# A recommender tower in one kernel: second feed-forward product with w_2 stationary in two 64-column tiles, its result copied and turned back; item/geo half of the fused layer in 64-column tiles

## The chip, the cores and the metric

The kernel runs on one core of one Trainium2 chip. The metric is device time in microseconds (us), the median of three runs. A program of this kind keeps five engines busy at once: TensorE (PE, with its weight loads as a row PEld of their own), VectorE (DVE), ScalarE (ACT), GpSimd (POOL) and SyncE (SP), which here only issues transfers.

## The reference, cut to what matters

128 sequences of 128 tokens go through three layers of width 64. Biases and constants are left out of this cut.

```python
item_emb, geo, visit = emb_table[ids], geo_table[ids], visit_table[ids]
cat = concat(gelu(item_emb @ w_item), gelu(geo @ w_geo), gelu(visit @ w_visit))
h = item_emb + 0.1 * layer_norm(gelu(cat @ w_fuse)) * (ids != 0)   # "fused layer"
h = h + attention(layernorm(h))                                     # 4 heads of 16
x = layernorm(h)
weights = x @ wr + br
sel = the 63 tokens of a sequence with the largest weights
y = gelu(sel @ w1 + b1) @ w2 + b2         # w1 64x256, w2 256x64
h = h + x + scatter(y * weights[sel])
```

The kernel computes `y` for every token and multiplies the rows that were not selected by a coefficient of zero.

## The kernel before, in words

The 128 sequences are taken in 32 groups of four (`GB`, `NG`). A group passes five stages, and step `i` of the program works on five groups at once: `a = i + 2` (gathered rows, item/geo/visit layers, fused layer), `b = i + 1` (layer norm, q, k, v), `c = i` (attention scores and exponentials), `e = i - 1` (attention values and output projection), `d = i - 2` (the feed-forward layer). Steps -2 to 3 and the last few are written out; those between are a hardware loop whose body is two steps, an even one and an odd one. There is no scheduler: each engine has its own written list of instructions per step, executes it strictly in that order, and the lists are tied by semaphores (`wait(engine, name, ...)`, `.then_inc`). So an instruction that waits holds back all that stands behind it on its engine.

What the lists hold around the change, in order:

- PE: transposes of the gathered rows (L903), of the visit rows (L911), the four score products of group c (L923), the item/geo product (L930), the visit product (L937), attention values in 32-column tiles (L867), the fused layer (L949 with `w_fv`, then two products L951 with `w_fe` and `w_fo`), transpose of x2 (L959), of the attention values (L876), of the row maxima `neg_max` (L967), q and k (L974, L979), transpose of x3 (L986), of the fused result (L999), first feed-forward product (L1009), v (L1016), transposed scores (L884, L886), transpose of the attention output (L819), second feed-forward product (`ffn_second`, L843), output projection (`project`, L833). Then comes the next step's L903.
- ACT: copies of the transposed rows (`ig_in` L462, `vi_in` L464), the gelus `cat` (L467) and `catv` (L470), the copy `pv_t` (L474), the gelu `fused` (L479), the copies `x2t` (L484) and `max_t` (L488), `q_mask` (L494), the copy `x3t` (L501), `k_hi` (L510), two gelus of the hidden layer `hid` (L516), then four exponentials `prob` (L523) with the copy `o_t` of the attention output (L455) behind the first of them.
- DVE: after the statistics of group a and the sum `W` (L775) it adds the bias to the feed-forward result and stores it (`ffn_out`, `Y`, L661), fetches indices (L677), adds the attention output to `R` (L682), then statistics, four maxima `neg_max` (L670), two normalisations `x` (L586), and so on without a break.

w_fe and w_fo are 128x128 matrices of which one half is zero: both products write all 128 partitions, and each adds only to its half. The second feed-forward product has the hidden values as stationary operand (128x128) and `w_2` as the moving one (64 columns), and its result stands with tokens on the partitions. An f32 product shows in the trace as two matmul rows; a transpose as one.

Of the kernel before, what the change touches and what calls it, by code (L numbers as in the profile page):

```python
# [32 lines left out]
ALU = mybir.AluOpType  # L33
# [33 lines left out]
    ("w_ig", P), ("w_vi", 2 * P), ("w_fe", P), ("w_fo", P), ("w_fv", P), ("w_2", 2 * D),  # L67
    ("w_o", D), ("ident", P),
    ("gamma", D), ("beta", D), ("bv", D), ("b2", D), ("wr", D), ("br", 1),
    ("b_ig", 1), ("b_vi", 1), ("b_fu", 1), ("b_q", 1), ("b_k", 1), ("b_1", 2), ("lo_row", 1),  # L70
# [8 lines left out]
def build(nc, ids, table, packed, out):  # L79
    with ExitStack() as ctx:  # L80
# [3 lines left out]
        def sem(name):  # L84
# [61 lines left out]
        hid = sb("hid", [P, 2, GT])  # L146

# [36 lines left out]
            "hid_ready", "f2_ready", "y_ready",  # L184
# [253 lines left out]
        def _(act):  # L438
# [18 lines left out]

            def step(i, odd, half):
# [46 lines left out]
                if on(b):  # L505
                    wait(act, "k_ready", 2, b)
                    if on(b - 2):
                        act.wait_ge(k_pair_in[1 - odd], (half + odd) * 64)
                    ends(act, "k_bd_in", 64, b - 2)
                    act.activation(by_row(k_hi[1 - odd][:, :]), two_banks(K_BANKS), ACT.Identity,  # L510
                                   bias=w["b_k"]).then_inc(S["kh_ready"], 1)
                if on(d):
                    ends(act, "f2_ready", 1, d - 1)
                    for m in range(2):
                        wait(act, "f1_ready", 4, d)
                        act.activation(by_row(hid[:, m, :]), two_banks((ffn_bank(d), ffn_bank(d) + 1), m),  # L516
                                       ACT.Gelu_apprx_tanh, bias=w["b_1"][:, m:m + 1]
                                       ).then_inc(S["hid_ready"], 1)
                for s in range(GB):
                    if on(c):  # L520
                        ends(act, "pv_ready", 1, c - 1)
                        wait(act, "st_ready", GB, c, s + 1)
                        act.activation(prob[:, s, :, :].rearrange("p h q -> p (h q)"),  # L523
                                       bank[SCORES[s]][:, :], ACT.Exp, scale=SCALE
                                       ).then_inc(S["prob_ready"], 1)
                    if s == 0 and on(e) and not late(i):
                        attention_out(e)

            pipeline(act, step)


        @block.vector
        def _(dve):
# [124 lines left out]
            def ffn_out(d):  # L658

                wait(dve, "f2_ready", 1, d)  # L660
                dve.tensor_tensor(  # L661
                    of(Y, d), bank[ffn_bank(d) + 1][:, 0:GB * D].rearrange("p (b d) -> p b d", b=GB),
                    w["b2"].unsqueeze(1).to_broadcast([P, GB, D]), ALU.add
                ).then_inc(S["y_ready"], 1)
# [144 lines left out]
        def _(pe):  # L809
# [28 lines left out]
            def ffn_second(d):  # L838

                wait(pe, "hid_ready", 2, d)  # L840
                for s in range(GB):
                    for m in range(2):
                        last = mm(bank[ffn_bank(d) + 1][:, s * D:(s + 1) * D],  # L843
                                  hid[:, m, slot(s)[0]], w["w_2"][:, m * D:(m + 1) * D],
                                  start=(m == 0), stop=(m == 1))
                last.then_inc(S["f2_ready"], 1)

# [44 lines left out]
            def step(i, odd, half):  # L892
# [53 lines left out]
                if on(a):  # L946
# [3 lines left out]
                    for n, wf in enumerate(("w_fe", "w_fo")):  # L950
                        last = mm(bank[6][:, 0:2 * P], w[wf],  # L951
                                  cat[:, :].rearrange("p (r s q) -> p s r q", r=2, s=2)[:, n],
                                  start=False, stop=(n == 1))
# [39 lines left out]
                if type(i) is int and i == NG + 1:  # L993
                    ffn_second(NG - 2)
                if on(a):
# [45 lines left out]
            ffn_second(NG - 1)  # L1041

# [57 lines left out]
```

## Time and profile before

| | before |
|---|---|
| median of 3 runs | 566.99 us (565.08, 566.99, 570.79) |
| the profiled execution | 564.28 us, of which the span is 562.5 us |
| PE / PEld busy | 86% / 67% |
| DVE busy | 83% |
| ACT busy | 73% |
| POOL busy | 61% |
| mean granted TensorE clock | 0.955 of 2.4 GHz |
| matmul rows | 4100 |

The span counts from the first to the last instruction of the profiled execution. Busy shares are averages over stages with different limits; a group of the timeline merges neighbouring instructions of one line, and the ends of matmuls are modelled, so that distances between starts are the safer reading on PE.

### The profile page before, as it was taken

The page shows a single profiled execution, that of the slowest core. Times are in us where ns is not written, and L with a number is a line of the kernel's source. Part 1 is how long each engine was busy: PE and PEld are TensorE (multiplying, and loading weights), DVE is VectorE, ACT ScalarE, POOL GpSimd, SP SyncE. Part 2 cuts the span into 40 slices and gives each one's busy share as a digit, 9 for nine tenths or more (in the row PEclk, how much of TensorE's full clock was granted, in tenths as well). Part 3 has the DMA queues.
Part 4 walks back from the last instruction along what each step waited for, and adds up shares of the span by engine and source line. Part 5 has one row for each costly group of instructions (what it writes and reads, how often), then busy time and mean ns, then how long its engine had stood idle before and what let it go on. Part 6 is the DMA issues. An engine that isn't in the chain of part 4 may idle for free.

```text
span 562.5 us, 14030 instructions
## 1 busy us (share of the span) xinstructions
PE 485.2 (86%) x4100; PEld 375.8 (67%) x4100; DVE 464.3 (83%) x1917; ACT 411.3 (73%) x694; POOL 342.1 (61%) x411
## 2 busy tenths in 40 slices
PE   0777788989898999999999999999999999977653
PEld 0445566767776777777777777777777777766443
DVE  5356576878798989899898989898989888898987
ACT  0326476888778888888889888888888788866830
POOL 5555365556566667666666666666766676432574
PEclk9989899899999999999999999999999999999855
DMA  3135545445555555555555555555554555444344
GB/s 102 23 69 114 96 108 102 94 94 104 110 103 98 108 109 110 114 111 112 112 115 102 109 105 112 110 111 107 107 105 101 110 113 112 105 94 96 76 112 113
DMA packets 89635, 57.74 MB, mean 103 GB/s; under 512 B 27408, under 2 KB 79248, under 8 KB 89488
## 3 DMA queue, kind: packets, MB, share of 16 engines
q1 hardware_dynamic: 83472, 47.55, 37.5%
q0 software_dynamic: 6144, 9.97, 12.4%
q8 instruction: 8, 0.13, 0.1%
q14 instruction: 11, 0.09, 0.1%
HBM read 11.08 MB, written 4.19 MB: 27 GB/s over the span
## 4 chain that ended last, share of the span: by engine, by line
PE 38%; DVE 20%; issue 19%; POOL 9%; ACT 8%; another core or an unknown queue 2%; DMA 1%; DVEq 1%; SPq 0%; ACTq 0%; POOLq 0%
PE psum L1009 5%; PE psum L930 4%; POOL rs L354 4%; PE psum L867 4%; DVE st L571 3%; PE psum L951 3%; PE psum L974 3%; PE psum L923 3%; POOL G L346 2%; PE psum L949 2%; DVE R L767 2%; PE psum L843 2%; ACT q_mask L494 2%; PE psum L903 2%
## 5 line engine op out<-in xcount | busy, mean ns | idle before, releaser
L354 POOL TENSOR_TENSOR rs<-ve,minus_half 128x4 f32<-128x4 f32 x96 | 99.6, 1037 | 130.9 <-DVE ve L581 120.3
L346 POOL DMA_INDIRECT G<-table,idx x128 | 125.5, 981 | 39.9 <-issue 35.2
L670 DVE TENSOR_REDUCE neg_max<-psum 128x4 f32<-128x512 f32 x128 | 84.3, 681 | 0.0
L523 ACT ACTIVATE prob<-psum 128x512 f32<-128x512 f32 x128 | 69.7, 611 | 0.5 <-PE psum L886 0.2
L586 DVE TENSOR_SCALAR x<-R,mv,rs 128x64 f32 (+1 forms) x256 | 66.2, 324 | 1.6 <-POOL rs L354 1.5
L843 PE MATMUL psum<-wt,hid 128*128 128x64 f32 x512 | 66.1, 285 | 0.0
L843 PEld LDWEIGHTS psum<-wt,hid 128*128 128x128 f32 x512 | 62.9, 200 | 0.5 <-ACT hid L516 0.2
L884 PE MATMUL psum<-max_row,ones_r 128*128 128x512 f32 x128 | 54.7, 428 | 0.0
L1009 PE MATMUL psum<-x3t,wt 64*128 64x256 f32 x256 | 40.1, 436 | 15.8 <-issue 8.9
L886 PEld LDWEIGHTS psum<-q_bd,k_pair 128*128 128x128 f32 x256 | 49.7, 194 | 5.8
L886 PE MATMUL psum<-q_bd,k_pair 128*128 128x256 f32 x256 | 51.9, 285 | 0.0
L728 DVE SCALAR_TENSOR_TENSOR q_s<-psum,wt,q_mask 128x512 fp32r<-128x512 f32 x32 | 24.0, 751 | 31.2 <-ACT q_mask L494 25.6
L516 ACT ACTIVATE hid<-psum,wt 128x512 f32<-128x512 f32 x64 | 40.6, 685 | 11.6 <-PE psum L1009 11.2
L516 ACT ACT_TABLE_LOAD x31 | 39.8, 1283 | 8.1 <-PE psum L1009 7.6
L571 DVE BATCH_NORM_STATS2 st<-R 128x6 f32 (+1 forms) x256 | 39.3, 216 | 3.9
L523 ACT ACT_TABLE_LOAD x32 | 41.1, 1283 | 1.9 <-PE psum L886 1.3
L930 PE MATMUL psum<-ig_in,wt 128*128 128x512 f32 x64 | 36.8, 658 | 4.9 <-DVE R L682 2.9
L1009 PEld LDWEIGHTS psum<-x3t,wt 64*128 64x128 f32 x256 | 24.0, 203 | 25.1 <-issue 14.4
L767 DVE SCALAR_TENSOR_TENSOR R<-t,rm,u 128x64 f32 (+1 forms) x128 | 35.1, 332 | 6.1 <-DVE rm L763 5.8
L923 PE MATMUL psum<-k_bd,q_s 128*128 128x512 f32 x128 | 38.9, 425 | 1.0 <-DMA k_bd<-k_hi 1.0
L479 ACT ACTIVATE fused<-psum,wt 128x256 f32<-128x256 f32 x32 | 15.2, 475 | 32.8 <-PE psum L951 27.7
L467 ACT ACT_TABLE_LOAD x30 | 38.5, 1283 | 0.5
(117 smaller groups left out, 1150.8 us busy)
## 6 DMA issues: line engine op xcount, KB each, us to landing
q_bd<-q_s SPq DMA_DIRECT2D x256, 64.0 KB
k_bd<-k_hi SPq DMA_DIRECT2D x128, 64.0 KB
k_pair<-k_hi SPq DMA_DIRECT2D x64, 128.0 KB
k_pair<-k_lo SPq DMA_DIRECT2D x64, 128.0 KB
out<-R SPq DMA_DIRECT2D x11, 256.0 KB, 2.6
G<-table,idx POOLq DMA_INDIRECT x128
wt<-packed SPq DMA_DIRECT2D x1, 1028.5 KB, 5.1
out<-R SPq DMA_DIRECT2D x2, 512.0 KB, 3.9
```

The costliest lines, as they stand in the source:

```text
L346: pool.indirect_dma_start(G[par][:, b, :], None, table, bass.IndirectOffsetOnAxis(ap=idx[par][:, b:b + 1], axis=0),).then_inc(gathered[par ...
L354: pool.tensor_tensor(rs[:, :], ve[:, :], minus_half[:, :], ALU.pow).then_inc(S[dst], 1)
L516: act.activation(by_row(hid[:, m, :]), two_banks((ffn_bank(d), ffn_bank(d) + 1), m), ACT.Gelu_apprx_tanh, bias=w["b_1"][:, m:m + 1]).then_ ...
L523: act.activation(prob[:, s, :, :].rearrange("p h q -> p (h q)"), bank[SCORES[s]][:, :], ACT.Exp, scale=SCALE).then_inc(S["prob_ready"], 1)
L571: last = dve.bn_stats(st[:, b, :], src(b))
L586: last = dve.tensor_scalar(dst[:, b, :], src(b), mv[:, b, 0:1], rs[:, b:b + 1], ALU.subtract, ALU.mult)
L670: dve.tensor_reduce(neg_max[:, HEADS * s:HEADS * s + HEADS], bank[SCORES[s]][:, :].rearrange("p (h k) -> p h k", h=HEADS), AX, ALU.max, ne ...
L843: last = mm(bank[ffn_bank(d) + 1][:, s * D:(s + 1) * D], hid[:, m, slot(s)[0]], w["w_2"][:, m * D:(m + 1) * D], start=(m == 0), stop=(m == 1))
L886: last = mm(bank[SCORES[s]][:, pair * 2 * P:(pair + 1) * 2 * P], k_pair[odd][:, pair, tok], q_bd[odd][:, at, pair, :, :].rearrange("p h q ...
L923: mm(bank[SCORES[s]][:, :], q_s[:, tok], k_bd[:, at, :, :].rearrange("p h k -> p (h k)"), start=True, stop=True).then_inc(S["s_ready"], 1)
L930: mm(bank[6][:, :], w["w_ig"], ig_in[:, :], start=True, stop=True).then_inc(S["ig_ready"], 1)
L1009: mm(bank[ffn_bank(d) + r][:, m * 2 * P:(m + 1) * 2 * P], w["w_1"][rows, m * P:(m + 1) * P], x3t[rows, :], start=True, stop=True, tile_pos ...
```

## The change

Three things, and what they need. First, `ffn_second` takes `w_2` as the stationary operand (64 columns) and the hidden values as the moving one (256 columns at a time), in two column tiles of the array: r = 0 writes partitions 0 to 63, r = 1 partitions 64 to 127. The result now has the features on the partitions. Second, ACT copies it into a new tile `y_t` and adds the bias there (`ffn_copy`), PE turns it back with two transposes (`ffn_back`), and DVE's `ffn_out` is a copy that waits for these. Third, the item/geo half of the fused layer uses one 128x64 matrix `w_f` in two column tiles in place of `w_fe` and `w_fo`. The packed constants shrink from 2057 to 1802 columns.

```diff
@@ act @@
+            def ffn_copy(d):
+                wait(act, "f2_ready", 1, d)
+                ends(act, "yb_ready", 1, d - 1)
+                act.activation(y_t[:, :], bank[ffn_bank(d) + 1][:, 0:2 * P], ACT.Identity,
+                               bias=w["b_2"]).then_inc(S["yt_ready"], 1)
...
                     if s == 0 and on(e) and not late(i):
                         attention_out(e)
+                    if s == 1 and on(d) and not late(i):
+                        ffn_copy(d)
@@ vector @@
             def ffn_out(d):
-                wait(dve, "f2_ready", 1, d)
-                dve.tensor_tensor(
-                    of(Y, d), bank[ffn_bank(d) + 1][:, 0:GB * D].rearrange("p (b d) -> p b d", b=GB),
-                    w["b2"].unsqueeze(1).to_broadcast([P, GB, D]), ALU.add
+                wait(dve, "yb_ready", 1, d)
+                dve.tensor_copy(
+                    of(Y, d), bank[ffn_bank(d) + 1][:, 0:GB * D].rearrange("p (b d) -> p b d", b=GB)
                 ).then_inc(S["y_ready"], 1)
@@ tensor @@
             def ffn_second(d):
                 wait(pe, "hid_ready", 2, d)
-                for s in range(GB):
-                    for m in range(2):
-                        last = mm(bank[ffn_bank(d) + 1][:, s * D:(s + 1) * D],
-                                  hid[:, m, slot(s)[0]], w["w_2"][:, m * D:(m + 1) * D],
-                                  start=(m == 0), stop=(m == 1))
+                for m in range(2):
+                    for r in range(2):
+                        last = mm(bank[ffn_bank(d) + 1][r * D:(r + 1) * D, 0:2 * P],
+                                  w["w_2"][:, m * D:(m + 1) * D],
+                                  hid[:, m, r * 2 * P:(r + 1) * 2 * P],
+                                  start=(m == 0), stop=(m == 1), tile_position=(0, r * D))
                 last.then_inc(S["f2_ready"], 1)
+            def ffn_back(d):
+                wait(pe, "yt_ready", 1, d)
+                for j in range(2):
+                    last = mm(bank[ffn_bank(d) + 1][:, j * P:(j + 1) * P],
+                              y_t[:, j * P:(j + 1) * P], ident, start=True, stop=True,
+                              is_transpose=True)
+                last.then_inc(S["yb_ready"], 1)
...
                     mm(bank[6][:, 0:2 * P], w["w_fv"], catv[:, :], start=True, stop=False)
-                    for n, wf in enumerate(("w_fe", "w_fo")):
-                        last = mm(bank[6][:, 0:2 * P], w[wf],
+                    for n in range(2):
+                        last = mm(bank[6][n * D:(n + 1) * D, 0:2 * P], w["w_f"],
                                   cat[:, :].rearrange("p (r s q) -> p s r q", r=2, s=2)[:, n],
-                                  start=False, stop=(n == 1))
+                                  start=False, stop=True, tile_position=(0, n * D))
...
                 if on(e) and not late(i):
                     project(e)
+                if on(d) and not late(i):
+                    ffn_back(d)
```

In the last steps (i = 32 and 33) the copy and the transposes stand directly behind the product, and the last group's `ffn_copy` and `ffn_back` end their engines' lists.

Where the new instructions stand on PE, at the end of a step in the loop. Before, with L819 the transposed attention output, L843 the second feed-forward product, L833 the projection and L903 the next step's first transposes:

```order
L819 MATMUL psum<-ident_bf,o 128x128 x3
L205 ISA
L843 MATMUL psum<-wt,hid 128x64 [waits hid_ready]
L843 MATMUL psum<-wt,hid 128x64 x7
L833 MATMUL psum<-wo_part,o_t 128x64 [waits o_t_ready]
L833 MATMUL psum<-wo_part,o_t 128x64 x11
```

The same place with the change, where L855 is the product, L845 the projection, L865 the transposes back and L925 what was L903:

```order
L855 MATMUL psum<-hid,wt 64x256 [waits hid_ready]
L855 MATMUL psum<-hid,wt 64x256 x3
L845 MATMUL psum<-wo_part,o_t 128x64 [waits o_t_ready]
L845 MATMUL psum<-wo_part,o_t 128x64 x11
L865 MATMUL psum<-wt,y_t 128x128 [waits yt_ready]
L865 MATMUL psum<-wt,y_t 128x128
L925 MATMUL psum<-wt,G 128x128 [waits v_out,gathered1]
L925 MATMUL psum<-wt,G 128x128 x3
```

Eight products of 64 columns became four of 256, and two transposes with a wait for ACT's copy now stand ahead of the next step's first instruction.

On ACT, at the end of a step in the loop, with the change (L533 is `prob`, L456 is `o_t`, L463 the new copy; before, the rows are the same without L463):

```order
L533 ACT_TABLE_LOAD
L533 ACTIVATE prob<-psum 128x512 [waits st_ready]
L456 ACTIVATE o_t<-psum 128x512 [waits ot_ready]
L206 REGISTER_ALU
L533 ACTIVATE prob<-psum 128x512 [waits st_ready]
L463 ACTIVATE y_t<-psum,wt 128x256 [waits f2_ready]
L206 REGISTER_ALU
L533 ACTIVATE prob<-psum 128x512 [waits st_ready]
```

The copy stands between the second and the third exponential, and no further table load comes with it.

On DVE, the same stretch of a step, with the change (L787 is the sum `W`, L674 what was L661, L689 and L694 what were L677 and L682):

```order
L787 TENSOR_REDUCE W<-xw 128x4
L674 REGISTER_ALU [waits yb_ready]
L674 COPY Y<-psum 128x256
L689 ISA
L689 COPY idx<-idx_all 128x4
L694 ISA [waits wo_ready]
L694 TENSOR_TENSOR R<-R,psum 128x256
```

Nothing moved there: the copy keeps the place of the addition, but the register instruction ahead of it waits for `yb_ready` (the transposes back) where it waited for `f2_ready` (the product).

## Rows read from the trace of the kernel before

**Rows 1.** The page, busy time of the engines: us, share, instructions.

```profile
PE 485.2 (86%) x4100; PEld 375.8 (67%) x4100; DVE 464.3 (83%) x1917; ACT 411.3 (73%) x694; POOL 342.1 (61%) x411
```

**Rows 2.** Timeline of ACT, 250 to 268 us: start us, us, instruction, [idle before <-releaser].

```profile
251.96 0.78 ACT L494 ACTIVATE q_mask<-psum,bq_lo,wt 128x512 fp32r<-128x512 f32 x1 [0.40 <-PE psum L974]
252.72 0.38 ACT L501 ACTIVATE x3t<-psum 128x256 f32<-128x256 f32 x1
...
255.60 1.27 ACT L516 ACTIVATE hid<-psum,wt 128x512 f32<-128x512 f32 x2 [0.61 <-PE psum L1009]
...
258.68 0.59 ACT L455 ACTIVATE o_t<-psum 128x512 bf16<-128x512 bf16 x1
259.15 1.58 ACT L523 ACTIVATE prob<-psum 128x512 f32<-128x512 f32 x3
260.63 0.60 ACT L462 ACTIVATE ig_in<-psum 128x512 f32<-128x512 f32 x1
...
265.47 0.48 ACT L479 ACTIVATE fused<-psum,wt 128x256 f32<-128x256 f32 x1 [0.86 <-PE psum L951]
...
267.05 0.78 ACT L494 ACTIVATE q_mask<-psum,bq_lo,wt 128x512 fp32r<-128x512 f32 x1 [0.55 <-PE psum L974]
```

**Rows 3.** Timeline of ACT, the following step, 267.5 to 283.5 us.

```profile
273.64 1.58 ACT L523 ACTIVATE prob<-psum 128x512 f32<-128x512 f32 x3
275.07 0.64 ACT L462 ACTIVATE ig_in<-psum 128x512 f32<-128x512 f32 x1
...
281.78 0.78 ACT L494 ACTIVATE q_mask<-psum,bq_lo,wt 128x512 fp32r<-128x512 f32 x1 [0.40 <-PE psum L974]
```

**Rows 4.** Timeline of PE, 250 to 268 us.

```profile
256.92 2.00 PE L843 MATMUL psum<-wt,hid 128*128 128x64 f32 x16
259.32 0.52 PE L833 MATMUL psum<-wo_part,o_t 65*128 65x64 bf16 x12 [0.40 <-ACT o_t L455]
259.94 0.65 PE L903 MATMUL psum<-wt,G 128*128 128x128 f32 x4
...
261.47 1.02 PE L930 MATMUL psum<-ig_in,wt 128*128 128x512 f32 x2
```

**Rows 5.** Timeline of PE, the following step, 267.5 to 283.5 us.

```profile
276.00 1.10 PE L930 MATMUL psum<-ig_in,wt 128*128 128x512 f32 x2 [0.16 <-DVE R L682]
...
277.47 1.08 PE L867 MATMUL psum<-prob,V 128*32 128x128 f32 x32
278.49 0.70 PE L949 MATMUL psum<-catv,wt 128*128 128x256 f32 x2
279.02 1.03 PE L951 MATMUL psum<-cat,wt 128*128 128x256 f32 x4
279.88 0.38 PE L959 MATMUL psum<-wt,x 128*128 128x128 f32 x2
280.10 0.60 PE L876 MATMUL psum<-wt,pv_t 128*128 128x128 f32 x4
280.75 0.33 PE L967 MATMUL psum<-wt,neg_max 128*128 128x128 f32 x1
```

**Rows 6.** Timeline of DVE, 250 to 268 us.

```profile
259.48 0.41 DVE L661 TENSOR_TENSOR Y<-psum,wt 128x256 f32 x1
...
264.21 1.28 DVE L670 TENSOR_REDUCE neg_max<-psum 128x4 f32<-128x512 f32 x2
```

**Rows 7.** Timeline of DVE, the following step, 267.5 to 283.5 us.

```profile
274.69 0.42 DVE L661 TENSOR_TENSOR Y<-psum,wt 128x256 f32 x1
...
279.41 1.28 DVE L670 TENSOR_REDUCE neg_max<-psum 128x4 f32<-128x512 f32 x2
```

**Rows 8.** Waits, whole span: engine, line <- releaser: us in total, times, longest.

```profile
DVE R L767 <- DVE rm L763: 5.8, 24, 0.2
```

**Rows 9.** Timeline of DVE, 500 to 563 us: the smallest copy out of PSUM nearby.

```profile
524.77 0.28 DVE L640 COPY coef<-psum 128x112 f32<-128x112 f32 x1 [0.41 <-PE psum L860]
```

**Rows 10.** The chain that ended last, 515 to 563 us: start us, us, what.

```profile
555.10 3.62 PE psum L843 x16
```

More of the change, by code:

```diff
@@ L66 @@
     ("w_q", P), ("w_k", P), ("w_v", P), ("w_1", HID),
-    ("w_ig", P), ("w_vi", 2 * P), ("w_fe", P), ("w_fo", P), ("w_fv", P), ("w_2", 2 * D),
+    ("w_ig", P), ("w_vi", 2 * P), ("w_f", D), ("w_fv", P), ("w_2", 2 * D),
     ("w_o", D), ("ident", P),
-    ("gamma", D), ("beta", D), ("bv", D), ("b2", D), ("wr", D), ("br", 1),
-    ("b_ig", 1), ("b_vi", 1), ("b_fu", 1), ("b_q", 1), ("b_k", 1), ("b_1", 2), ("lo_row", 1),
+    ("gamma", D), ("beta", D), ("bv", D), ("wr", D), ("br", 1),
+    ("b_ig", 1), ("b_vi", 1), ("b_fu", 1), ("b_q", 1), ("b_k", 1), ("b_1", 2), ("b_2", 1), ("lo_row", 1),
 ]
@@ L146, in build @@
         hid = sb("hid", [P, 2, GT])
+        y_t = sb("y_t", [P, 2 * P])
         wt_rank = sb("wt_rank", [P, P])
@@ L183, in build @@
             "xw_ready", "w_ready", "r_ready", "x3t_ready", "x3t_out", "f1_ready",
-            "hid_ready", "f2_ready", "y_ready",
+            "hid_ready", "f2_ready", "yt_ready", "yb_ready", "y_ready",
         )}
@@ L511, in step @@
                                    bias=w["b_k"]).then_inc(S["kh_ready"], 1)
+                if type(i) is int and i == NG + 1:
+                    ffn_copy(NG - 2)
                 if on(d):
@@ L527, in step @@
                         attention_out(e)
+                    if s == 1 and on(d) and not late(i):
+                        ffn_copy(d)
             pipeline(act, step)
+            ffn_copy(NG - 1)
         @block.vector
@@ L994, in step @@
                     ffn_second(NG - 2)
+                    ffn_back(NG - 2)
                 if on(a):
@@ L1041, in _ @@
             ffn_second(NG - 1)
+            ffn_back(NG - 1)
 def kernel(x, L0_tok_emb_table, L0_tok_geo_table, L0_tok_visit_table, L0_tok_w_item,
@@ L1070 @@
     wf = np.asarray(L0_tok_w_fuse)
-    c["w_fe"][:, :D] = c["w_fo"][:, D:] = wf[:P]
+    c["w_f"][:] = wf[:P]
     c["w_fv"][:D, :D] = c["w_fv"][D:, D:] = wf[P:]
@@ L1076 @@
     for n, src in (("gamma", L0_tok_ln_gamma), ("beta", L0_tok_ln_beta), ("bv", L0_attn_bv),
-                   ("b2", L0_ffn_b2), ("wr", L0_ffn_wr), ("br", L0_ffn_br)):
+                   ("wr", L0_ffn_wr), ("br", L0_ffn_br)):
         c[n][:] = np.asarray(src).reshape(1, -1)
     c["b_ig"][:D, 0], c["b_ig"][D:, 0] = np.asarray(L0_tok_b_item), np.asarray(L0_tok_b_geo)
-    for n, src in (("b_vi", L0_tok_b_visit), ("b_fu", L0_tok_b_fuse)):
+    for n, src in (("b_vi", L0_tok_b_visit), ("b_fu", L0_tok_b_fuse), ("b_2", L0_ffn_b2)):
         c[n][:D, 0] = c[n][D:, 0] = np.asarray(src)
```

## Prediction

> **What bounds the kernel now.** I first read the busy times of the page. PE is busy for 86% of the span, DVE for 83%, ACT for 73% [rows 1]. No engine is full, so the bound is a ring of waits, and the timelines of ACT, PE and DVE over two steps of the loop show it. The start of `q_mask` on ACT marks a step: 251.96, 267.05 and 281.78 us [rows 2, 3]. A "long" step takes 15.09, the "short" one behind it 14.73, a pair 29.82.
>
> From `q_mask` on ACT works nearly without a break to the `ig_in` of the next step. The one break is 0.61 ahead of `hid` in the long step [rows 2]. In the long step PE has finished the second feed-forward product (L843) and waits 0.40 for `o_t`; then follow L833, L903 at 259.94 and L930 at 261.47 [rows 4]. In the short step L930 waits for DVE's `R` (L682), which stands behind `Y` [rows 5, 7]. From L930 on PE's list runs through L867, L949 and L951, and `q_mask` starts 1.09 after DVE's last `neg_max` ends in the short step (279.41 + 1.28 = 280.69, then L967 at 280.75 and `q_mask` at 281.78) [rows 3, 5, 7]. So the ring is ACT from `q_mask` to `o_t`, then PE from L833 to L974, with DVE from `Y` to `neg_max` beside it and nearly as long. L843 lies beside ACT's work, not on the ring.
>
> **The second product.** An L843 row costs about 0.11: 16 of them take 2.00 with the last one's modelled end of 0.27 [rows 4]. A row of 256 moving columns costs 0.215: four L951 rows take 279.88 - 279.02 = 0.86. That column tiles run together is seen in L867: 32 rows of 128 columns take 278.49 - 277.47 = 1.02, so four tiles share eight slots of 0.11 (the spacing within L876, (0.60 - 0.27) / 3), and 0.14 is left over for changing the tiles [rows 5]. A change back also exposes a weight load: two L949 rows take 0.53, not 0.43 [rows 5]. The new product has eight rows, four slots of 0.215, so 0.86 + 0.14 + 0.14 = 1.14 against 1.84. PE saves 0.70, and pays two transposes, 0.11 each and 0.05 for the exposed first load, 0.27 together. Of the 0.70 the ring gets nothing: L833 waited for `o_t` already in the long step, and `o_t` does not come earlier.
>
> **The copy on ACT.** `y_t` reads 256 columns with a bias. The trace has no such copy; it lies between `x3t` (256 columns without bias, 0.38) and `fused` (256 with bias, a gelu, 0.48) [rows 2]. I take 0.48, since it has the bias too. The product will be ready at about 258.4, and the copy's turn comes after the second exponential: exponentials start 0.48 apart ((275.07 - 273.64) / 3 [rows 3]), so in the long step at 259.15 + 0.48 = 259.63. It is not late itself, but it starts only there, ends at 260.11, and the last two exponentials, `ig_in` and all behind them on ACT move by 0.38 (`q_mask` is followed by `x3t` after 0.76 of its 0.78, so 0.02 to 0.10 of an instruction is overlapped).
>
> **The wait on PE.** The transposes back start 0.05 after the copy, as L833 does after `o_t` (258.68 + 0.59 to 259.32), so at 260.16. L903 follows at 260.43 against 259.94, 0.49 later, and L930 0.49 later too [rows 4]. Queued behind the waiting transposes is everything of the next step on PE. ACT's `ig_in`, which needs L903, comes at the same time by either way (0.38 from ACT, 0.49 from PE).
>
> **The wait on DVE.** The second transpose starts at 260.32 and ends 0.27 later at 260.59. DVE is told after 0.05, and a register instruction stands between the wait and the copy. Where DVE has such a hand-over to itself, it costs 5.8 / 24 = 0.24 [rows 8]; I take 0.15 for both, and 0.05 to 0.24 as the bounds. So `Y` starts at 260.74, not 259.48: 1.26 later [rows 6]. In the short step the copy starts at 273.64 + 0.48 = 274.12, the transposes at 274.65, `Y` at 275.23, not 274.69: 0.54 later [rows 3, 7]. Queued behind it are `idx`, `R`, the statistics, the four maxima and both normalisations, with no idle time to take it up. `Y` as a copy instead of an addition may be cheaper than 0.41. Bounds: nothing saved, and 0.13 saved (the copy of 112 columns took 0.28 [rows 9]); I take 0.06.
>
> The Trainium skill ("VectorE: DVE Perf Modes", Why PSUM operands drop a tier) says that an f32 operand in PSUM keeps an operation at the basic rate, so a copy would save nothing. By it the sum below would be 29 x 0.06 = 1.7 higher; no row here shows a copy of this size.
>
> **The fused layer.** Four rows in 0.86 become two slots, 0.43, with 0.14 for going into the tiles and 0.14 for coming out: L959 comes 0.15 earlier, and the last product, which `fused` waits for, 0.29 earlier [rows 5]. In the loop this is worth nothing: PE reaches L967 earlier relative to L930, but `neg_max` is later still. In the four steps ahead of the first feed-forward group it is worth about 0.2 each, 0.8.
>
> **The sum.** Long step: `neg_max` ends at 264.21 + 1.28 + 1.26 - 0.06 = 266.69 [rows 6]; 1.09 later, at 267.78, comes `q_mask`, which was at 267.05: +0.73. Short step: 0.54 - 0.06 = +0.48. A pair is 1.21 longer, a step 0.605. Groups 0 to 28 meet it in the steps 2 to 30: 29 x 0.605 = 17.5. Less 0.8 for the first steps. At the end the last product, 3.62 for 16 rows at the low clock [rows 10], becomes eight slots' worth in four, 1.8 and 0.2, but 0.05 + 0.48 + 0.05 for the copy and about 0.9 for two transposes and their end come behind it: 3.5 against 3.6, nothing. The constants are 12% smaller, but PE's first instruction waits for gathered rows: nothing. Together +16.7, from 564.3 (span 562.5 and 1.8 around it) to 581.0. The median of the runs of before, 566.99, stands 2.7 above that execution, so I name 583.
>
> **Rivals.** (1) *Only PE's leg is left*: the transposes back are served so early, or `Y` is so quick, that DVE never sets L967. Then the ring is PE's: +0.49 less 0.28 for the earlier `fused` in the long step, and L903 at 274.92 with L930 1.53 behind it (as 261.47 - 259.94) at 276.45, +0.45 - 0.28 in the short one. That is 0.38 a pair, 5.5 in all, less 0.8: 569 on the profile's clock, 571.5 for the median. Against it: DVE has no idle time between `Y` and `neg_max`. (2) *Faster*: ACT takes the copy up in the 0.86 that it idles ahead of `fused` [rows 2], PE's shorter lists then pull the ring in by the 0.28 of `fused` each step: 29 x 0.28 + 0.8 = 8.9 less, 558. It decides itself at 0.28: if the copy and its waits add less than this to a step's way from `o_t` to L930, the change gains. For it: ACT is only 73% busy. Against it: the idle time lies behind L949, the copy ahead of L903, and the path between holds 0.49. (3) *The stall ahead of `hid` spreads*: 0.61 stands there in each long step only, laid to L1009 [rows 2]. With everything shifted it could stand in the short steps too: 14.5 x 0.6 = 8.7 more, 592. (4) *The column tiles of 64 do not overlap*: 0.43 more for L951 and 0.86 more for the second product, which has over 1 us in hand. L967 would then be set by PE, some 0.15 later a step: 4 more, 587. L867 speaks against it.
>
> **How the numbers follow.** My forecast has 0.55, rival 3 0.15, rival 4 0.1, rival 1 0.13, rival 2 0.07. The bounds of the unknown costs move the forecast: the hand-over to DVE by -0.1 to +0.09 a step (-2.9 to +2.6), `Y` by +1.7 to -2.0, `y_t` of 0.38 by -2.9. The range from 571 to 591 reaches to rival 1 and nearly to rival 3 and leaves out rival 2 and the rest. About 1% (5.7 us) is what a measurement of this kernel can tell from no change. Slower by more: the forecast, rivals 3 and 4 and a part of rival 1, 0.83. Within: 0.1. Faster: 0.07.
>
> **What the changed profile would show.** ACT: one more instruction of about 0.48 between the exponentials, no further table load, and no wait ahead of it. PE: a wait for ACT's `y_t` ahead of the transposes, L925 some 0.5 later after `o_t`, the second product in about 1.1. DVE: idle time ahead of `Y` of roughly 1.2 and 0.5 in turn, laid to PE's transposes, and none to speak of before. `neg_max` as the releaser of PE's transpose of the maxima in every step. A pair of steps 31.0 long. If `Y` doesn't wait, the DVE term is wrong; if `fused` comes earlier and `q_mask` with it, rival 1 or 2 holds.

## The result and the profile after

| | before | after |
|---|---|---|
| median, measured on one chip | 568.89 us (565.08 to 579.14, 4 runs) | 624.06 us (621.85 to 626.10, 4 runs) |
| ratio | | 1.108, 95% interval 1.103 to 1.114 |
| profiled execution | 564.28 us, span 562.5 us | 624.87 us, span 623.1 us |
| mean granted clock | 0.955 | 0.907 |

The ratio leaves out executions more than 1.5% above the fastest of the same kernel (of before, the one of 579.14), here and below; the medians keep them. The change costs 55 us where 16 were forecast: the direction was right, and the size lies far outside the range. The page of after, its busy times and its row of the granted clock, against [rows 1]:

```profile
PE 499.3 (80%) x3908; PEld 337.6 (54%) x3908; DVE 463.3 (74%) x1917; ACT 425.2 (68%) x726; POOL 341.5 (55%) x411
PEclk9999898797999889998999899879798998798765
```

PE is busier in microseconds (499 against 485) although it has 192 rows fewer. The clock row goes with that: it falls to 7 and 8 tenths again and again up to the end.

The table of stretches puts a number to it. Its columns are the stretch, its length, busy time and rows of PE, PEld, DVE, ACT and POOL, the mean granted clock, DMA share and GB/s. Before, then after:

```profile
113.00:500.00 387.00, 367.54 (x3281) 288.81 (x3283) 342.07 (x1465) 326.81 (x540) 250.20 (x303) 1.00 0.53 107
```

```profile
113.00:560.00 447.00, 385.65 (x3154) 264.96 (x3154) 341.41 (x1470) 339.94 (x568) 249.39 (x303) 0.92 0.47 93
```

Between two starts of `q_mask` on ACT, from the seventh step on, there are 25 steps. Before they take 375.1 us, 15.01 each. After, 18 of them take 285.2 (15.84 each) and 7 take 147.0 (21.0 each). So of 57.0 us, 25 x 0.83 = 21 are spread over all steps, and 7 x 5.16 = 36 are in seven long ones. The 3.6 left of the 60.6 between the two profiled executions lie ahead of these steps and behind them. Nine of the 18 hold some half clock too and still last 15.6 to 16.9. The forecast had 0.605 a step and no long ones.

**One of the seven**, 268.88 to 289.88 us. The clock by stretches, the step's low ones in the second and fourth row (3.4 us at 0.52 and at 0.53, which is the level of 1.2 GHz):

```profile
272.00:278.20 6.20, 4.50 (x44) 3.26 (x42) 4.05 (x17) 5.46 (x9) 3.97 (x6) 1.00 0.63 137
278.20:281.60 3.40, 3.40 (x9) 1.98 (x8) 3.23 (x19) 2.04 (x3) 1.40 (x2) 0.52 0.52 111
281.60:288.40 6.80, 4.03 (x50) 2.52 (x48) 3.37 (x12) 2.38 (x5) 4.55 (x5) 0.99 0.40 66
288.40:291.80 3.40, 3.18 (x14) 1.95 (x14) 1.23 (x3) 1.54 (x5) 0.00 (x0) 0.53 0.08 12
```

PE's timeline of after in this step, and behind the line of dots four of the same rows in the next one, whose clock is whole from 292 us on and which is undisturbed in these rows:

```profile
273.90 1.08 PE L855 MATMUL psum<-hid,wt 128*64 128x256 f32 x8
276.24 0.52 PE L845 MATMUL psum<-wo_part,o_t 65*128 65x64 bf16 x12 [1.25 <-ACT o_t L456]
277.08 0.44 PE L865 MATMUL psum<-wt,y_t 128*128 128x128 f32 x2 [0.32 <-ACT y_t L463]
277.65 0.65 PE L925 MATMUL psum<-wt,G 128*128 128x128 f32 x4
278.17 1.89 PE L945 MATMUL psum<-k_bd,q_s 128*128 128x512 f32 x4
279.86 1.91 PE L952 MATMUL psum<-ig_in,wt 128*128 128x512 f32 x2
282.21 1.08 PE L889 MATMUL psum<-prob,V 128*32 128x128 f32 x32
286.63 0.66 PE L898 MATMUL psum<-wt,pv_t 128*128 128x128 f32 x4 [1.76 <-issue]
...
298.89 1.17 PE L945 MATMUL psum<-k_bd,q_s 128*128 128x512 f32 x4
299.89 1.02 PE L952 MATMUL psum<-ig_in,wt 128*128 128x512 f32 x2
301.29 1.08 PE L889 MATMUL psum<-prob,V 128*32 128x128 f32 x32
303.79 0.60 PE L898 MATMUL psum<-wt,pv_t 128*128 128x128 f32 x4
```

Read it from the top. The new second product (L855) takes 1.08 where the old one took 2.00, and behind it PE idles 1.25 for `o_t` and 0.32 for `y_t`; before it idled 0.40 at the same place [rows 4]. Then the clock is at half: L952 starts 1.69 behind L945 instead of 1.00, and its two rows take 1.91 instead of 1.02. L889 starts 4.04 behind L945, not 2.40: PE is 1.6 late.

What comes next on GpSimd, and then on ACT, after again; the last ACT row is that of the undisturbed step:

```profile
282.42 1.08 POOL L347 DMA_INDIRECT G<-table,idx  x1 [0.19 <-issue]
...
286.31 0.95 POOL L347 DMA_INDIRECT G<-table,idx  x1 [0.30 <-issue]
```

```profile
285.98 0.60 ACT L482 ACTIVATE pv_t<-psum 128x512 f32<-128x512 f32 x1 [3.12 <-remote]
287.40 0.47 ACT L487 ACTIVATE fused<-psum,wt 128x256 f32<-128x256 f32 x1 [0.83 <-remote]
...
302.44 0.60 ACT L482 ACTIVATE pv_t<-psum 128x512 f32<-128x512 f32 x1 [0.26 <-PE psum L889]
```

L889's rows end at 283.3, and `pv_t`, which needs only them, starts at 285.98. Meanwhile GpSimd issues its four indirect transfers, the "burst" (282.42 to 287.26), and `pv_t` starts as the third of them ends (286.01). In the undisturbed step L889 ends at 302.37, before the burst that starts at 303.05, and `pv_t` follows 0.07 later. So the late L889 meets the burst and `pv_t` comes 2.6 later behind it (the idle time of 3.12 holds PE's lateness too). The long step takes 20.99, the undisturbed one 15.59. Of the 5.4 between them 0.3 is gone by the start of L945, 1.6 is the half clock up to L889, 2.6 the burst, and 0.9 lies between `pv_t` and the next `q_mask`, where the second low stretch begins (288.4 to 291.8, behind 2.9 of idle time of PE).

The table of waits of after, then two lines of before that answer to them (engine and line, total us, times, longest):

```profile
ACT pv_t L482 <- remote: 31.0, 9, 5.1
DVE Y L674 <- PE psum L865: 29.3, 30, 2.4
PE psum L845 <- ACT o_t L456: 28.8, 27, 1.3
```

```profile
PE psum L833 <- ACT o_t L455: 5.7, 13, 0.8
ACT pv_t L474 <- remote: 3.6, 1, 3.6
```

The wait for `o_t` stood in 13 steps with 0.44 each before and stands in 27 with 1.07 each after. From the seventh step on it is 1.1 to 1.3 in the steps of after that have a stall of 0.6 ahead of `hid`, and 0.4 to 0.7 in those with none. "Remote" is a releaser that the trace can't name.

### The profile page after: what moved, and what is told of

It reads as the page before. It is cut to its first block, busy times and chain, and to the rows that moved or that the text cites. A ratio compares the mean times of both kernels' runs of the same rounds, so it can differ in the third digit from the quotient of the medians.

```text
span 623.1 us, 13683 instructions
## 1 busy us (share of the span) xinstructions
PE 499.3 (80%) x3908; PEld 337.6 (54%) x3908; DVE 463.3 (74%) x1917; ACT 425.2 (68%) x726; POOL 341.5 (55%) x411
## 3 DMA queue, kind: packets, MB, share of 16 engines
q0 software_dynamic: 6144, 9.97, 11.4%
## 4 chain that ended last, share of the span: by engine, by line
PE 42%; ACT 19%; issue 17%; DVE 9%; another core or an unknown queue 6%; POOL 4%; DMA 1%; DVEq 1%; ACTq 0%; SPq 0%; POOLq 0%
PE psum L1032 8%; PE psum L945 4%; PE psum L996 4%; ACT hid L526 4%; PE psum L952 4%; ACT prob L533 4%; ACT L533 3%; PE psum L1001 2%; PE psum L889 2%; PE psum L865 2%; DVE neg_max L682 2%; PE psum L925 2%; PE psum L1008 2%; ACT y_t L463 2%
## 5 line engine op out<-in xcount | busy, mean ns | idle before, releaser
L682 DVE TENSOR_REDUCE neg_max<-psum 128x4 f32<-128x512 f32 x128 | 84.3, 681 | 0.0
L533 ACT ACTIVATE prob<-psum 128x512 f32<-128x512 f32 x128 | 73.5, 612 | 0.7 <-PE psum L908 0.4
L740 DVE SCALAR_TENSOR_TENSOR q_s<-psum,wt,q_mask 128x512 fp32r<-128x512 f32 x32 | 24.0, 751 | 35.2 <-ACT q_mask L502 24.8
L1032 PE MATMUL psum<-x3t,wt 64*128 64x256 f32 x256 | 43.3, 464 | 7.2 <-issue 4.4
L482 ACT ACTIVATE pv_t<-psum 128x512 f32<-128x512 f32 x32 | 19.1, 597 | 42.5 <-remote 31.0
L945 PE MATMUL psum<-k_bd,q_s 128*128 128x512 f32 x128 | 45.9, 489 | 0.9 <-DMA k_bd<-k_hi 0.9
L952 PE MATMUL psum<-ig_in,wt 128*128 128x512 f32 x64 | 40.1, 714 | 1.8 <-ACT ig_in L470 1.8
L845 PE MATMUL psum<-wo_part,o_t 65*128 65x64 bf16 x384 | 16.9, 194 | 28.8 <-ACT o_t L456 28.8
L502 ACT ACTIVATE q_mask<-psum,bq_lo,wt 128x512 fp32r<-128x512 f32 x32 | 24.9, 777 | 21.8 <-PE psum L996 21.1
L898 PE MATMUL psum<-wt,pv_t 128*128 128x128 f32 x128 | 20.8, 287 | 20.9 <-issue 15.6
```

Of the source, the lines that this page charges most:

```text
L682: dve.tensor_reduce(neg_max[:, HEADS * s:HEADS * s + HEADS], bank[SCORES[s]][:, :].rearrange("p (h k) -> p h k", h=HEADS), AX, ALU.max, ne ...
L945: mm(bank[SCORES[s]][:, :], q_s[:, tok], k_bd[:, at, :, :].rearrange("p h k -> p (h k)"), start=True, stop=True).then_inc(S["s_ready"], 1)
L952: mm(bank[6][:, :], w["w_ig"], ig_in[:, :], start=True, stop=True).then_inc(S["ig_ready"], 1)
L1032: mm(bank[ffn_bank(d) + r][:, m * 2 * P:(m + 1) * 2 * P], w["w_1"][rows, m * P:(m + 1) * P], x3t[rows, :], start=True, stop=True, tile_pos ...
```

## The experiments

Three theories. A: the long steps come from the clock, and the clock from the work taken off PE ahead of `o_t`. B: the long steps are a matter of the longer ring alone, or of the new wait ahead of the transposes. C: the 0.8 in every other step is the forecast's ring and, beside it, rival 3 (the stall ahead of `hid` in both steps). The kernel before is measured anew beside each group of runs; only the ratios can be set side by side from one group to another.

**The two halves of the change apart.** The fused layer alone, on the kernel before:

```diff
-                    for n, wf in enumerate(("w_fe", "w_fo")):
-                        last = mm(bank[6][:, 0:2 * P], w[wf],
+                    for n in range(2):
+                        last = mm(bank[6][n * D:(n + 1) * D, 0:2 * P], w["w_f"],
                                   cat[:, :].rearrange("p (r s q) -> p s r q", r=2, s=2)[:, n],
-                                  start=False, stop=(n == 1))
+                                  start=False, stop=True, tile_position=(0, n * D))
```

> The kernel before with the fused layer's change alone. Theory (clock): what costs 55 us is a TensorE that is idle more and whose clock then falls, together with the stalls of PE's semaphores that follow; this part takes only 0.15 us of PE's time out of a step, behind no wait, so the clock stays up between 120 and 520 us and the time is 558 to 568, some 0 to 8 us faster than before, since `fused` comes 0.29 us earlier and L967 is set by PE in every second step. Rival (tiles): the switches into and out of the 64-column tiles cost more than they save, and the time is 3 to 10 us longer.

Measured 569.91 against 564.55, ratio 1.003 (0.997 to 1.010): no difference that shows. The clock didn't stay whole as expected: the traced execution has one stretch of 6.8 us at half clock, from 328.9 us, behind 2.9 of idle time of PE ahead of L1009, in a step of 18.93.

The feed-forward part alone is the same edit taken back in the changed kernel.

> The changed kernel with the fused layer put back to w_fe and w_fo. Theory (clock): the second product, the copy on ACT and the transposes back carry the whole loss: 615 to 630 us, mean granted clock about 0.90 to 0.92, slow steps of about 21 us in between steps of 15.7. Rival (both parts needed): with 0.15 us more of PE work a step the clock stays up, the time is about 590 and the clock 0.95.

Measured 620.90 against 564.55, ratio 1.093 (1.084 to 1.102), clock 0.909. The feed-forward part carries the loss. The fused layer shows no worth either way.

**Give PE its work back, in idle time.** The changed kernel with the product, and the projection behind it, each computed twice into the same place:

```diff
+                for again in range(2):
+                    for s in range(GB):
+                        for n in range(3):
+                            last = mm(wo_bank(e)[:, s * D:(s + 1) * D],
...
+                for again in range(2):
+                    for m in range(2):
+                        for r in range(2):
+                            last = mm(bank[ffn_bank(d) + 1][r * D:(r + 1) * D, 0:2 * P],
```

> The changed kernel with the second feed-forward product computed twice over (0.86 us more PE work a step) and the output projection twice over (0.35 us more), both in places where PE waits for ACT; the second pass writes the same values. Theory (clock): PE is busy where it was idle, the clock stays up from about 120 us on, no step takes 21 us, and the time falls to 585 to 595 though PE does more. Rival (plain work): the clock has nothing to do with it, the stalls come from the order of waits; the time is 624 or, by the added work, up to 640.

Measured 583.94 against 564.55, ratio 1.035 (1.030 to 1.041). More work on PE makes the changed kernel 40 us faster (620.90 with the feed-forward part alone in the same group; 585 to 595 had been expected here). The stretch from 160 to 480 us, after and then this kernel:

```profile
160.00:480.00 320.00, 275.32 (x2272) 188.69 (x2269) 247.39 (x1063) 243.62 (x410) 183.57 (x222) 0.93 0.48 95
```

```profile
160.00:480.00 320.00, 306.23 (x2882) 213.53 (x2880) 268.25 (x1161) 268.33 (x447) 203.34 (x246) 1.00 0.51 104
```

```profile
PE psum L846 <- ACT o_t L456: 10.2, 23, 1.0
```

The clock is whole again, the wait for `o_t` is 0.44 where it stands, and no step is longer than 16.1 once the first five are past.

**Take work off PE and do nothing else.** The kernel before, with one of the two halves of the second product left out:

```diff
-                    for m in range(2):
+                    for m in range(1):
...
-                                  start=(m == 0), stop=(m == 1))
+                                  start=True, stop=True)
```

> The kernel before with one of the two halves of the second feed-forward product left out (the result misses half the hidden layer): 0.9 us less PE work a step, ahead of the wait for `o_t`, and no other change. Theory (clock): lighter PE alone brings the clock down in some windows; the time is 590 to 610 with slow steps as in the changed kernel, mean clock 0.92. Rival (the waits are to blame, ACT's copy and PE's wait for it): the product was hidden, the time stays within 3 us of before, clock 0.95.

Measured 586.09 against 564.55. The four times are 567.05, 584.39, 587.80 and 602.38, with a mean clock of 0.950, 0.925, 0.923 and 0.903, and the eleven of before lie between 560.70 and 571.08. So one execution lost nothing, three lost 20 to 38 us, and with such a spread there is no ratio; the clock falls in some executions and not in others. In the traced one (584.39) it is 0.95 from 160 to 480 us. No copy, no transposes, no wait ahead of them, and the long steps are there. One of 21.2 us, its timeline of PE, GpSimd's last transfer, and ACT:

```profile
318.22 1.10 PE L843 MATMUL psum<-wt,hid 128*128 128x64 f32 x8
320.62 0.52 PE L833 MATMUL psum<-wo_part,o_t 65*128 65x64 bf16 x12 [1.30 <-ACT o_t L455]
321.25 1.09 PE L903 MATMUL psum<-wt,G 128*128 128x128 f32 x4
322.21 2.05 PE L923 MATMUL psum<-k_bd,q_s 128*128 128x512 f32 x4
...
329.47 0.95 POOL L346 DMA_INDIRECT G<-table,idx  x1 [0.30 <-issue]
...
331.30 0.60 ACT L474 ACTIVATE pv_t<-psum 128x512 f32<-128x512 f32 x1 [4.79 <-remote]
```

The same picture: a short L843, an idle time of 1.30, then four rows of L923 in 2.05 where the same product takes 1.17 at full clock (L945 above), the burst (325.58 to 330.42), and `pv_t` 4.4 behind the end of L867's rows at 326.87. As a theory of all long steps B falls: neither the longer ring nor the wait ahead of the transposes is needed for one.

**Which idle time.** Only the product twice, and only the projection twice:

> The changed kernel with the second product computed twice, the projection once. PE's wait of 1.25 for `o_t` shrinks to 0.4, the wait of 0.33 ahead of the transposes back stays. Theory (the place where the product became short decides): no low stretch after 120 us, 580 to 587 us as with both computed twice. Rival (the two waits add up and each matters): a few slow steps, 590 to 610.

> The changed kernel with the projection computed twice, the product once: the wait ahead of the transposes back is filled, the wait of 1.25 for `o_t` stays. Theory (the short product decides): slow steps as in the changed kernel, 610 to 626. Rival (the wait ahead of the transposes decides): no slow steps, 580 to 587.

Against 565.11, the product twice gives 584.93 (1.038, 1.030 to 1.046), the projection twice 612.49 (1.085, 1.071 to 1.100). Their stretches, product first:

```profile
160.00:480.00 320.00, 300.33 (x2638) 206.76 (x2640) 267.94 (x1159) 267.75 (x445) 202.90 (x245) 1.00 0.52 104
```

```profile
160.00:480.00 320.00, 282.29 (x2548) 195.03 (x2546) 251.96 (x1083) 250.15 (x418) 189.24 (x228) 0.96 0.49 97
```

The place ahead of `o_t`, which the product fills, decides, and the 0.33 ahead of the transposes doesn't. Whether filling the latter lessens the loss isn't shown: the interval reaches from 1.071 to 1.100, and the feed-forward part alone, with that wait left open, has 1.084 to 1.102. Nor is the wait for `o_t` enough to bring the clock down each time. With the projection twice PE waits 1.1 to 1.3 in each of the seven steps from 112.7 to 222.9 us with the clock whole, and it falls only in the eighth:

```profile
113.00:222.00 109.00, 98.25 (x932) 68.74 (x930) 91.05 (x395) 91.69 (x153) 68.90 (x84) 1.00 0.51 105
222.00:244.00 22.00, 17.75 (x143) 11.90 (x142) 14.77 (x63) 13.68 (x24) 12.63 (x15) 0.89 0.49 88
```

**The copy's place and its price on ACT.** In the changed kernel, the copy directly behind `o_t` instead of one exponential later:

```diff
-                    if s == 1 and on(d) and not late(i):
+                    if s == 0 and on(d) and not late(i):
                         ffn_copy(d)
```

> The changed kernel with the copy `y_t` one exponential earlier on ACT, directly behind `o_t`. By the accounts of the prediction the transposes back then stand ready when the projection ends, L925 is hardly later than L903 was, `Y` is 0.8 later in one step and 0 in the next, and a pair of steps is 0.3 longer than before; with the stall ahead of `hid` in every step 0.9. At full clock that is 567 to 577 us. Theory (the idle time of PE brings the clock down): PE still waits 1.25 for `o_t` where the product became short, so some windows stay low: 580 to 605 us, clock 0.92 to 0.94, fewer slow steps than the changed kernel. Rival (the wait ahead of the transposes alone brought it down): no slow steps, 567 to 577.

Measured 582.26 (575.61 to 583.92) against 567.95, ratio 1.022 (1.013 to 1.032). The stretch's clock is 0.99. This is the lowest ratio of the whole change with the real gather, and the wait for `o_t` is still 24.8 us in 28 times, so that wait alone doesn't fix what the clock does. The same kernel, and the product and the projection twice:

> As the run before it, and with the second product and the projection computed twice (1.2 us more PE work a step in PE's idle places). Theory (clock): no low stretch after 120 us, steps of 15.2 to 15.4 on the mean against 15.8 of the run with the copy in its first place: 570 to 580 us. Rival (the place of the copy does not matter): 584 as there.

Measured 582.57, ratio 1.025 (1.019 to 1.031): a miss, 2.6 us above what was expected. The steps are 15.4 and 15.8, because the stall ahead of `hid` stands in nearly each of them, where the run before had it in half.

The copy alone, on the kernel before: 256 columns of `hid`, into a tile that nobody reads, behind the second exponential:

```diff
+                    if s == 1 and on(d) and not late(i):
+                        wait(act, "hid_ready", 2, d)
+                        act.activation(y_t[:, :], hid[:, 0, 0:2 * P], ACT.Identity,
+                                       bias=w["b_q"]).then_inc(S["yt_ready"], 1)
```

> The kernel before with one more copy of 256 columns with a bias on ACT (out of `hid`, into a tile that nobody reads) behind the second exponential. It prices ACT's term alone: PE and DVE wait for nothing new. By the accounts ACT's 0.38 moves `ig_in`, `cat` and `catv`, of which 0.05 to 0.25 is taken up by PE's wait ahead of L949: a step is 0.15 to 0.33 longer, 5 to 10 us in all, 569 to 574, clock 0.95. Rival (ACT is the ring by itself): 0.38 a step, 11 us, 575. Rival (any delay brings the clock down): 590 or more with slow steps.

Measured 575.29 against 567.95, ratio 1.013 (1.007 to 1.020). The copy costs 7.3 us in its place even if nobody waits for it. That lies within the 5 to 10 us that were expected, but the interval is 3.8 to 11.4 us and doesn't rule out the rival's 11.

**Without the bursts.** SyncE fetches fixed rows of the table in one plain transfer in place of GpSimd's four indirect ones, in the kernel before and in the changed one:

```diff
-                for b in range(GB):
-                    pool.indirect_dma_start(
-                        G[par][:, b, :], None, table,
...
+                sp.dma_start(G[par][:, :, :],
+                             table[0:GT, :].rearrange("(p b) f -> p b f", b=GB)
+                             ).then_inc(gathered[par], 16)
```

> The kernel before with GpSimd's four indirect transfers of a group replaced by one plain transfer of 512 fixed table rows, issued by SyncE; the gathered rows are then the wrong ones, all later work is the same. Theory (GpSimd's burst holds back PE's semaphores): the 0.61 ahead of `hid` in every second step is gone, and those steps last 14.5 to 14.7 instead of 15.1; 550 to 560 us. Rival (the stall comes from the order of PE's own work or of SyncE's transfers): it stays in every second step, 565.

> The changed kernel with the same replacement of the gather. Theory (burst): no 0.61 ahead of `hid`, and where the clock is low the step lasts 17 to 18 instead of 21, since ACT's `pv_t` no longer waits 3 us for a product that PE has issued long before: about 590 us with low stretches of the clock still there. Rival (the 21 us are the low clock alone): slow steps keep their 21 us. Second rival (the low stretches come from the burst too): no low stretch after 120 us, 575.

The kernel before without bursts takes 545.48 (2 runs), the changed one without bursts 555.72 (8 runs), and the full kernel before 549.34 in this group: ratios of 0.988 (0.974 to 1.003) and 1.014 (1.010 to 1.018). The change costs 10.2 us here. Two things stand apart from what was expected. The full kernel before is 15 to 20 us faster in this group than in the others, on a chip where it took 567.95 in the group before, and against it the plain transfer gains nothing that shows. And the theory had the changed kernel at 590 with low stretches left; it was the second rival (the low stretches come from the burst too) whose clock came true. ACT's timeline, without bursts, changed kernel: two steps, 14.92 and 15.36 long.

```profile
251.26 0.78 ACT L508 ACTIVATE q_mask<-psum,bq_lo,wt 128x512 fp32r<-128x512 f32 x1 [0.40 <-PE psum L1002]
254.29 1.27 ACT L532 ACTIVATE hid<-psum,wt 128x512 f32<-128x512 f32 x2
...
266.18 0.78 ACT L508 ACTIVATE q_mask<-psum,bq_lo,wt 128x512 fp32r<-128x512 f32 x1 [0.40 <-PE psum L1002]
269.21 1.27 ACT L532 ACTIVATE hid<-psum,wt 128x512 f32<-128x512 f32 x2
...
281.54 0.78 ACT L508 ACTIVATE q_mask<-psum,bq_lo,wt 128x512 fp32r<-128x512 f32 x1 [0.40 <-PE psum L1002]
```

Its stretch and its two waits that matter:

```profile
160.00:480.00 320.00, 291.59 (x2583) 202.07 (x2580) 277.53 (x1205) 278.88 (x467) 125.41 (x168) 1.00 0.48 107
```

```profile
PE psum L851 <- ACT o_t L462: 22.3, 31, 1.3
DVE Y L680 <- PE psum L871: 20.1, 30, 2.4
```

No stall ahead of `hid` in any step, `pv_t` laid to PE's product in all 32, no long step, and the clock whole from 40 to 490 us. PE has the same short product, but waits only 0.65 for `o_t` where it waits 1.25 in the long step above: that is the wait of the steps without the stall in the changed kernel too (0.4 to 0.7).

What the stall is worth can be read too, across groups, since no trace of the full kernels was taken in this one. The long step of the kernel before, 15.09 [rows 2], is 14.58 without bursts, its short one stays (14.73 and 14.68). The changed kernel's steps without bursts are 15.36 and 14.92. With bursts and PE filled they are 15.97 and 15.56, 0.61 and 0.64 more, and the stall ahead of `hid` stands in each. ACT's rows of that kernel:

```profile
258.29 1.27 ACT L526 ACTIVATE hid<-psum,wt 128x512 f32<-128x512 f32 x2 [0.61 <-PE psum L1034]
...
274.28 1.27 ACT L526 ACTIVATE hid<-psum,wt 128x512 f32<-128x512 f32 x2 [0.63 <-PE psum L1034]
```

So theory C holds. A pair of steps without bursts goes from 29.26 to 30.28, which is the ring, +1.02. The stall in both steps makes it 31.53. Before had it in one, 29.82. The net is 1.71 a pair: 1.02 from the ring and 0.69 from the spread stall. Not all steps keep to these pairs: over the 25 steps from the seventh on the changed kernel with PE filled takes 15.71 a step, 0.70 more than the 15.01 of before, where the pairs make it 0.86.

**The ring, last test.** The changed kernel without bursts and with the copy behind `o_t`:

> The changed kernel with the plain transfer in place of the gather (the rows are the wrong ones) and the copy `y_t` directly behind `o_t`. Against the same kernel with the copy in its first place (a pair of steps 30.3), the accounts of the prediction make a pair about 0.9 shorter, since `Y` starts about 0.48 earlier in each step: 29.4 to 29.7, some 545 to 549 us on a chip where that kernel took 555.7. Rival (ACT's time alone sets the pair, not DVE's): it stays at 30.2 or more, since ACT has as much to do as there.

Measured 546.38, with pairs of 14.88 and 14.67, 29.55 together. That is 0.73 less than with the copy one exponential later, as expected (29.4 to 29.7), and DVE's wait ahead of `Y` falls from 20.1 us to 3.8. With bursts and PE filled the copy's place is worth less, 31.53 against 31.2 a pair. The gather of fixed rows makes it no rival of the real kernels.

This run also closes a gap. It belongs to the group of the two runs with product or projection twice, where the kernel before took 565.11 and the stall of 0.6 stands ahead of `hid` in most steps. Without bursts it is gone there too, but for one wait at the start (its table of waits, then the stretch):

```profile
ACT hid L532 <- PE psum L1038: 2.9, 1, 2.9
```

```profile
160.00:480.00 320.00, 298.07 (x2659) 204.96 (x2655) 287.01 (x1240) 282.62 (x475) 129.22 (x172) 1.00 0.49 110
```

So the stall goes with the bursts, and not with the chip or the hour. The product is short here, PE waits 0.65 for `o_t` in the regular steps, and the clock stays whole.

No form of the change beats the kernel before. The nearest is the fused layer alone, which can't be told from it.

## Why the prediction was wrong in size

**The ring: about right.** It was forecast at 1.21 a pair and is 1.02. The forecast was a long step of 15.82 (15.09 + 0.73) with the stall ahead of `hid` in it, and a short one of 15.21 (14.73 + 0.48) without. Put together from two kernels, the long step with its stall is 15.97 (PE filled) and the short one without 14.92 (no bursts), 30.89 against 31.03; no run has this pair. The short one is less because the way from `Y` to the last `neg_max` isn't rigid. It was 4.72 before [rows 7], and is 303.09 - 298.72 = 4.37 in after's undisturbed step, where DVE's copy of the indices takes 0.16 (0.51 before). In the long step that copy is short too, but it and `R` start 0.58 and 0.83 behind `Y` instead of 0.34 and 0.40, and the way is 4.83. The wait itself was as said: in after's long step `Y` is 8.76 behind `q_mask`, 7.52 before, 1.24 later where 1.26 was taken. In the short one it is 8.17 behind `q_mask` without bursts, 7.58 in the kernel before without bursts, 0.59 later where 0.54 was taken.

**The single prices: right.** `y_t` takes 0.49 (taken 0.48). The product takes 1.08 by its rows (taken 1.14). The transposes start 0.84 behind L845 (taken 0.84), and L925 1.12 behind it in the short step and 1.41 in the long one (taken 1.11 there). `Y` as a copy costs 0.42:

```profile
298.72 0.42 DVE L674 COPY Y<-psum 128x256 f32 x1 [0.70 <-PE psum L865]
```

It saves nothing, where 0.06 was taken. By the Trainium skill ("VectorE: DVE Perf Modes", Why PSUM operands drop a tier), as quoted with the forecast, nothing was to be saved, and the trace agrees: 0.42 against 0.41 and 0.42 for the addition [rows 6, 7].

**Rival 3: it came, with 0.15 on it.** It was priced at 8.7 us. It is 0.69 a pair, at most 10 us. What failed is that "with everything shifted it could stand in the short steps too" stayed a chance, with no look at what makes the stall. That look was to be had: in after, `q_mask` at 305.47 and the burst's last transfer at 306.93, 1.46 later, go with a stall of 0.66, and `q_mask` at 289.88 with the last transfer at 286.31, long past, with none. In before it stands where the last transfer starts 1.47 behind `q_mask`, not where it starts 1.00 behind. In before, after and the two kernels with the product twice the stall of 0.6 goes with a distance of 1.45 to 1.48 in all but a few steps. The distance is no full rule: in the kernel with the copy alone it stands at 1.14 and 1.23 too, and with the copy early it is missing in single steps at 1.46.

Ring and spread stall together, with the clock up, are 584 to 585 us (the two runs with the product twice). That this is next to the forecast's 583 is luck: the forecast reached it from a median 2 us higher, with a ring 0.19 a pair too long, and without the stall. (Its own sum, 581.0 and 2.7, is 583.7.)

**The 40 us: the step that failed.** It is the sentence "PE saves 0.70 ... Of the 0.70 the ring gets nothing: L833 waited for `o_t` already". It costs a shortened, hidden product at zero, as idle time of an engine that is not waited for. The sum never asked what PE's idle time does to PE's own clock, though [rows 10] had a product at the low clock and the page a clock row. What the runs put in its place: with PE's work ahead of `o_t` at its old length the clock is whole from 160 to 480 us (before; product twice, 4 executions within 584.5 to 587.9), with the new form it is 0.93, and with half of L843 gone and nothing else changed it is 0.95 in the traced execution. A low stretch over L945 and L952 is then worth 1.6 us of PE's time by itself, 2.6 more because the late L889 meets the burst, and this comes seven times. The price has two conditions, neither of which was in the sum: the short product, and the bursts, without which the same short product brings no fall between 40 and 490 us.

The Trainium skill ("TensorE: Matmul & The Clock Gate", A second HAM failure mode: psum-queue depth-cycling) describes a kernel in which short idle times of PE between groups of matmuls make the clock swing between its two levels. The rows agree in kind: 1.25 and 0.32 idle, then 0.52 of the full clock.

**The other rivals.** Rival 4 is wrong: the product's eight rows fit 1.08, so the tiles of 64 do overlap. Rival 1 is wrong: DVE waits for the transposes in 30 steps, and a pair is 1.7 longer, not 0.4. Rival 2 is wrong: nothing gains, not even with the copy early and no bursts (a pair of 29.55 against 29.26 in the kernel before without bursts). The edit to the fused layer shows no gain, as said.

**Open.** How a burst of indirect transfers keeps ACT from going on behind PE isn't shown: the trace shows only that `pv_t` and `hid` wait past PE's rows when the burst is on, and that these waits are gone with it. What exactly makes the clock fall is open too. With the copy behind `o_t` PE waits 0.89 for `o_t` in 28 steps and the clock falls only twice between 120 and 500 us, and without bursts it waits 0.72 in 31 and the clock doesn't fall between 40 and 490 us. Whether idle time as such or its place in the step counts was not tested. Nor need a fall in mid-run belong to the change: the fused layer alone had one, and single executions of the kernel before, without a trace, took 578.72 and 581.20 us at a mean clock of 0.937 and 0.933.

## What to carry to other kernels

Work of PE that is hidden in a wait can be what keeps its clock up, as it was here. Before shortening it, ask how long PE will then idle, price a clock at 1.2 GHz in what follows it, and test the question for a few lines by computing the hidden product twice. A stall whose length doesn't fit its releaser's end (here 0.61 ahead of `hid`) should be followed to what else runs at that moment, since it moves and multiplies with any shift. A copy in a full in-order queue costs its own time and its place: one exponential earlier was worth 0.73 us in each pair of steps without bursts and 0.3 with them.

## What the hardware showed that was not expected

- TensorE at half clock (granted 0.52) in stretches of 3.4 us, behind an idle time of 1.25 and one of 0.32 us, in a kernel that keeps PE busy for 80% of the span. Computing a product of 1 us twice removed every such stretch between 160 and 480 us and 40 us of the time. Without the indirect transfers no such stretch came either, with the product short.
- While GpSimd issues four indirect transfers (4.8 us), ACT takes up PE's product 2.7 us after its last row (283.3 to 285.98), in the kernel with half the product left out 4.4 us. Without the indirect transfers the longest wait for a PE product at this place is 1.8 us.
- Four column tiles or two, the array runs them together: eight rows of 256 columns in two tiles of 64 take 1.08 us, sixteen 1.95 (product twice). One after the other at 0.215 each, eight would take 1.72.
